# A four-layer kernel on one core: the next norm's transposes moved from TensorE to eight DMAs, and the first two up products of an element done together

## What is computed

```python
x = x + (ctx @ Wo + bo)                 # end of the first pass; x2 below
h = _ln(x) * g2 + beta2                 # h2 below: "the next norm"
ff = _gelu2(h @ W1 + b1) @ W2 + b2      # 512 -> 2048 -> 512; first half of the steps
x = x + ff                              # x3 below

h = gelu(x @ Wi[e] + bi[e])             # layer 3, weights of expert e of the element
r = h @ Wo[e] + bo[e] + x               # second half of the steps
y = norm(r) * gamma[e] + beta[e]        # f below

Af, Bf = A_grid * y, B_grid * y         # layer 4: a stencil step on the 512 x 512 grid
out = max(y + dt * (-grad(Af) + 0.5 * grad2(Bf)), 0)
```

## Time and profile before

| | us |
|---|---|
| median of three timed runs | 2524.64 |
| lowest, highest | 2522.03, 2525.68 |
| the profiled execution | 2522.23 |
| span from its first to its last instruction | 2520.4 |
| TensorE busy, share | 2471.3, 98% |
| VectorE busy, share | 1904.1, 76% |
| ScalarE busy, share | 1126.5, 45% |
| GpSimd busy, share | 981.1, 39% |
| TensorE in the chain that ended last | 52% |

### The profile page before, as it was taken

How to read it: one execution, slowest core, us unless ns; L and a number is a source line. 1 busy time by engine, 2 the same in 40 slices (tenths; PEclk the granted TensorE clock), 3 DMA queues, 4 the chain that set the end, 5 groups by cost and what they waited for, 6 DMA issues and landing times.

```text
span 2520.4 us, 45559 instructions
## 1 busy us (share of the span) xinstructions
PE 2471.3 (98%) x14444; PEld 1221.4 (48%) x14444; DVE 1904.1 (76%) x3666; ACT 1126.5 (45%) x2159; POOL 981.1 (39%) x840
## 2 busy tenths in 40 slices
PE   7999999999999999999999999999999999999997
PEld 5555555555555555544444444444444444444443
DVE  7878777777777685763588689678787886986777
ACT  3666767675758585742223223233222322232231
POOL 1464646464646464410044143242341440531331
PEclk9999999999999999999999999999999999999999
DMA  7444444544544445451232142133222322321341
GB/s 244 140 154 155 152 156 152 164 153 151 166 149 161 148 151 169 159 193 51 72 126 84 62 135 92 59 117 117 84 87 92 105 84 75 125 92 59 114 140 53
DMA packets 150228, 311.35 MB, mean 124 GB/s; under 512 B 16619, under 2 KB 21739, under 8 KB 150004
## 3 DMA queue, kind: packets, MB, share of 16 engines
q1 hardware_dynamic: 140788, 291.93, 35.4%
q10 hardware_dynamic: 9216, 16.78, 1.8%
HBM read 291.68 MB, written 16.81 MB: 122 GB/s over the span
## 4 chain that ended last, share of the span: by engine, by line
PE 52%; DVE 3%; issue 1%; ACT 0%; POOL 0%; DVEq 0%; ACTq 0%
PE bank L1522 17%; PE bank L1524 16%; PE bank L1523 16%; PE bank L1508 1%; PE bank L1598 1%; DVE g2T_hi L1857 1%; DVE g2T_lo L1858 1%; PE bank L1528 0%; DVE w_hi L1933 0%; ACT g L1690 0%; DVE stage L1820 0%; DVE stage L1801 0%; PE bank L1644 0%; PE bank L1632 0%; DVE w_lo L1933 0%
## 5 line engine op out<-in xcount | busy, mean ns | idle before, releaser
L1109 DVE CUSTOM_DVE_ANT_0 w_words<-bank,stage 128x512 f32<-128x512 f32 x512 | 323.8, 686 | 102.0 <-PE bank L702 93.7
L884 ACT ACTIVATE w_words<-w_words,nmax 128x512 f32<-128x512 f32 x512 | 363.6, 714 | 42.1 <-DVE nmax L1109 41.0
L564 POOL TENSOR_TENSOR stage<-stage,mask_add 128x1024 f32<-128x1024 f32 x128 | 273.1, 2144 | 230.1 <-DMA stage<-in_bias 213.2
L1857 DVE CAST g2T_hi<-g 128x512 f16<-128x512 f32 x256 | 178.8, 698 | 221.0 <-ACT g L1690 217.1
L725 PE MATMUL bank<-ident,w_words 128*128 128x128 f32 x2048 | 298.3, 280 | 11.6 <-DVE late L1124 5.9
L725 PEld LDWEIGHTS bank<-ident,w_words 128*128 128x128 f32 x2048 | 222.8, 140 | 170.8 <-issue 82.9
L1690 ACT ACTIVATE g<-bank,bi 128x512 f32<-128x512 f32 x128 | 88.0, 687 | 352.3 <-PE bank L1524 331.3
L1858 DVE TENSOR_TENSOR g2T_lo<-g,g2T_hi 128x512 f16<-128x512 f32 x256 | 238.7, 933 | 8.8
L1432 POOL TENSOR_TENSOR stage<-grid,f 128x512 f32<-128x512 f32 x84 | 141.3, 1708 | 195.5 <-DVE f L1760 74.0
L870 ACT ACTIVATE late<-bank 128x512 f32<-128x512 f32 x256 | 150.9, 590 | 147.4 <-PE bank L725 147.2
L1866 DVE SCALAR_TENSOR_TENSOR wl_lo<-stage,wl_hi 128x1024 f16<-128x1024 f32 x128 | 196.6, 1536 | 6.8 <-ACT wl_hi L1702 6.6
(11 more groups left out here) (299 smaller groups left out, 4894.8 us busy)
## 6 DMA issues: line engine op xcount, KB each, us to landing
stage<-in_bias SPq DMA_DIRECT2D x256, 512.0 KB, 4.4
stage<-in_W_l SPq DMA_DIRECT2D x128, 512.0 KB, 3.4
grid<-in_grids SPq DMA_DIRECT2D x140, 256.0 KB, 3.6
xin<-in_x SPq DMA_DIRECT2D x32, 256.0 KB, 4.1
x_rows<-w_words ACTq DMA_DIRECT2D x32, 256.0 KB, 3.7
out<-stage ACTq DMA_DIRECT2D x32, 256.0 KB, 2.0
late<-x_rows SPq DMA_DIRECT2D x7, 1024.0 KB, 8.3
l_rows<-in_rows SPq DMA_DIRECT2D x8, 768.0 KB, 6.2
```

Of the source, the lines that this page charges most:

```text
L564: pool.tensor_tensor(bias[:, n % NB, :, :], bias[:, n % NB, :, :], mask_add[:, u % T, :].unsqueeze(1).to_broadcast([P, 2, S]), ALU.add).th ...
L884: act.activation(tile, tile, ACT.Exp, scale=-1.0, bias=nmax[:, u % 2, i:i + 1], accum_out=rsum[:, j, h:h + 1]).then_inc(prob_ready, 1)
L1109: dve.tensor_tensor_reduce(tiles[:, 4 * (u % NR) + i, :], bank[:, :], bias[:, half % NB, i % 2, :], -1.0, 3.0e38, ALU.add, ALU.min, nmax[: ...
L1857: link(dve.tensor_copy(gT[0][:, n % 4, :], g32[:, n % 2, :]))
```

## The change

The transposes of `h2` are taken from TensorE and given to DMAs that transpose on the way from SBUF to SBUF.

- ScalarE makes the high half of `h2` in rows, in float16, in steps 26 and 27 (two row tiles each), VectorE the low half in steps 27 and 28. They lie in `stage`, where `prod` lies (`h2_halves`).
- SP, at the end of its sequence for the element, waits for these and for the end of `up(31)` (the last reader of `xT`), and issues eight transposing DMAs: the four row tiles of the high half, then the four of the low half. Each moves 128 x 512 values of 16 bit. Each half has its own semaphore.
- The ring loses the four `h2T` entries.
- TensorE does `down(28)` to `down(31)` all after `up(31)`. Before, `down(28)` and `down(29)` stood behind `up(30)` and `up(31)`.
- TensorE does `up(0)` and `up(1)` of the next element together (`first_ups`): after the high halves are there, the 16 products that need only `xT` high, 8 for each bank; after the low halves are there, the 4 products with `xT` low for `up(0)` and then the 4 for `up(1)`.
- GpSimd waits for both halves before it writes `prod`.
- Semaphores are merged (`zeroed` into the new one of the split).

```diff
@@ end of SP's sequence(it)
+                if not is_last(it):
+                    sp.wait_ge(h2_split_and_zeroed, 1 + it * T + T)
+                    arrived(sp, it, ("up", STEPS - 1))
+                    sp.sem_inc(carrier, 1)
+                    for half in range(2):
+                        for t in range(T):
+                            sp.dma_start(xT[half][:, :, t * P:(t + 1) * P], h2_halves[half][:, t, :], transpose=True)\
+                                .then_inc(h2T_in[half], 16)
@@ GpSimd
                 if not is_first(it):
+                    for half_in in h2T_in:
+                        pool.wait_ge(half_in, it * 64)
                     for t in range(T):
                         alpha_products(pool, it - 1, t)
@@ TensorE
-                            elif not is_first(it):
-                                pe.wait_ge(h2T_split, it * C)
...
+                def first_ups():
+                    ws = [[[x[:, c, n * P:(n + 1) * P] for x in w1] for c in range(C)] for n in range(2)]
+                    first = [claim(pe, it, ("up", n)) for n in range(2)]
+                    pe.wait_ge(h2T_in[0], it * 64)
+                    for n in range(2):
+                        for c in range(C):
+                            pe.matmul(first[n][:, :], ws[n][c][0], xT[0][:, c, :], start=c == 0, stop=False)
+                            pe.matmul(first[n][:, :], ws[n][c][1], xT[0][:, c, :], start=False, stop=False)
+                    pe.wait_ge(h2T_in[1], it * 64)
+                    for n in range(2):
+                        for c in range(C):
+                            mm = pe.matmul(first[n][:, :], ws[n][c][0], xT[1][:, c, :], start=False, stop=c == C - 1)
+                        mm.then_inc(full_of(("up", n)), 1)
...
                     for n in range(half * NF, half * NF + NF):
-                        up(n)
-                        if n - LAG_DOWN >= half * NF and not (is_last(it) and n - LAG_DOWN >= STEPS - KEPT):
+                        if n == 0 and not is_first(it):
+                            first_ups()
+                        if n > 1 or is_first(it):
+                            up(n)
+                        if half * NF <= n - LAG_DOWN < STEPS - KEPT:
                             down(n - LAG_DOWN)
...
-                    if half:
-                        pe.wait_ge(h2_ready, it * T + T)
-                        for c in range(C):
-                            h2_transposes(claim(pe, it, ("h2T", c)), c).then_inc(full_of(("h2T", c)), 1)
-                    for n in range(half * NF + NF - LAG_DOWN, half * NF + NF):
+                    for n in range(STEPS - KEPT if half else NF - LAG_DOWN, half * NF + NF):
                         down(n)
@@ ScalarE
-                for c in range(0 if is_last(it) else C):
-                    copy_hi(("h2T", c), c)
+                    if n in (NORM2 + 3, NORM2 + 4) and not is_last(it):
+                        if n == NORM2 + 3:
+                            act.wait_ge(y_done, 1 + it * T)
+                            if is_first(it):
+                                act.wait_ge(w_split, len(PIECES))
+                        for t in range(2 * (n - NORM2 - 3), 2 * (n - NORM2 - 2)):
+                            act.wait_ge(h2_ready, it * T + t + 1)
+                            act.activation(h2_halves[0][:, t, :], h2[:, t, :], ACT.Copy).then_inc(hi_done, 1)
@@ VectorE
+                    if n in (NORM2 + 4, NORM2 + 5):
+                        for t in range(2 * (n - NORM2 - 4), 2 * (n - NORM2 - 3)):
+                            dve.wait_ge(hi_done, it * (C + T) + C + t + 1)
+                            dve.wait_ge(h2_ready, it * T + t + 1)
+                            dve.tensor_tensor(h2_halves[1][:, t, :], h2[:, t, :], h2_halves[0][:, t, :], ALU.subtract)\
+                                .then_inc(h2_split_and_zeroed, 1)
                 if is_last(it):
                     return
-                for c in range(C):
-                    lo_of(("h2T", c), C + c, c, h2T_split)
```

More of the change, by code:

```diff
@@ L1192, in ffn_pass @@
             in_ring(("L3", STENCIL[n]))
-    for c in range(C):
-        in_ring(("h2T", c))
     banks = Banks(order)
@@ L1217, in ffn_pass @@
         h2 = sb("h2", [P, T, D], F32)
+        h2_halves = [stage[:, 2 + i, :].bitcast(F16).rearrange("p (t d) -> p t d", t=T) for i in range(2)]
         f = sb("f", [P, T, D], F32)
@@ L1244, in ffn_pass @@
         ident_set = sem("ffn_ident_set")
-        zeroed = sem("zeroed")
         x2_in = sem("x2_in")
@@ L1253, in ffn_pass @@
         hi_done = sem("ffn_hi_done")
-        h2T_split = sem("h2T_split")
+        h2_split_and_zeroed = sem("h2_split_and_halo_zeroed")
+        h2T_in = [sem("h2T_hi_in"), sem("h2T_lo_in")]
         x3T_split = sem("x3T_split")
@@ L1310, in claim @@
             k = last[1]
-            signal, per = {"h2T": (h2T_split, C), "x3T": (x3T_split, C), "up": (gelu_ready, STEPS),
+            signal, per = {"x3T": (x3T_split, C), "up": (gelu_ready, STEPS),
                            "L3": (sum_ready, T)}[last[0]]
@@ L1396, in load_halo @@
                     sp.wait_ge(alpha_done, it * T)
-                    sp.wait_ge(zeroed, 1)
                     for k, part in enumerate((*vsp, *msp)):
@@ L1454, in _ @@
                                pattern=[[-1, P]], channel_multiplier=1).then_inc(ident_set, 1)
-            pool.memset(halo[:, :, :].rearrange("p t d -> p (t d)").bitcast(F32), 0.0).then_inc(zeroed, 1)
+            pool.memset(halo[:, :, :].rearrange("p t d -> p (t d)").bitcast(F32), 0.0).then_inc(h2_split_and_zeroed, 1)
             pool.wait_ge(cols_in, 16 * len(cols))
@@ L1524, in three @@
                 return pe.matmul(out, w[1], x[0], start=False, stop=last)
-            def h2_transposes(bank, c):
-                for t in range(T):
-                    mm = pe.transpose(bank[:, t * P:(t + 1) * P], h2[:, t, c * P:(c + 1) * P], ident[:, :])
-                return mm
             pe.wait_ge(sh["hT_split"], (B + 1) * C)
@@ L1837, in lo_of @@
                 def lo_of(key, k, c, signal):
-                    dve.wait_ge(hi_done, it * 2 * C + k + 1)
+                    dve.wait_ge(hi_done, it * (C + T) + k + 1)
                     dve.tensor_tensor(xT[1][:, c, :], psum[banks.place[key][0]][:, :], xT[0][:, c, :], ALU.subtract)\
```

## The result

The changed kernel takes 2532.47 us against 2524.71 us for the kernel before, medians of eight runs each made side by side: a ratio of 1.0032, 95% interval 1.0020 to 1.0043. It is slower, by 7.8 us. One of the changed kernel's eight runs fell in a slow state at a lower clock (3724.94 us); ratio and interval are of the fast ones, and the seven alone have a median of 2532.35 us, 7.6 above. The prediction was 2523.5 us and no measurable change; the change came out slower by a cost that stands in none of its steps. The time lies inside the stated range of 2514 to 2558 us, but the range reached so far up for low halves that come late, and TensorE never waited for them: that it holds is luck. The profiled execution took 2531.22 us, with a span of 2529.4 us, 9.0 more than before.

The account below looks back on a forecast made before the run. TensorE was taken as the bound, busy 2471.3 of 2520.4 us. Six boundaries at -0.02 us and the last at -0.97 summed to -1.1 us, from 2524.64 to 2523.5 us; range 2514 to 2558 us.

Parts of the forecast that it names:

- step (1): At seven element boundaries the 16 transposes leave TensorE: -1.75 us each, -12.2 us if nothing else moved.
- steps (2) and (3): Moving down(28) and down(29) behind up(31), and the h2 copies to steps 26 to 28, costs nothing.
- step (4): On SP, weight chunks and grids queued behind the transposes still land in time for their users; no cost.
- step (5): After up(31), high halves land at 4.2 us and low ones at 6.7, before they are wanted: no wait.
- halo row: Profile row of an SBUF-to-SBUF copy, 0.59 us to issue, 1.7 to landing, taken as the transposing DMAs' price.
- first rival: SP's transposes do not overlap, low halves come 4.6 us late at each boundary: +32 us, 2556 us; chance 0.26.
- steps (6) and (7): up(0) fills 1.73 us later, delaying down(2) by 1.73 at six boundaries and 0.78 at the last.
- The shift is absorbed: Rival: VectorE has room for up(0)'s later completion, so the transposes' gain stays: 2511 us; chance 0.09.
- either of the two new waits: Sign of being wrong: TensorE standing in first_ups for the high or the low halves; no wait was forecast.

Follow-up runs that it names:

- e6: Changed kernel with TensorE's loop head at slot 16, first loads ahead of the transposes, up(0)'s low products right after its eight high ones: 2510.78 us, ratio 0.9954.
- e1: Changed kernel with only the head of TensorE's loop put back at slot 16 of a code block: 2527.16 us, ratio 1.0012.
- e2: Kernel before, without transposing DMAs, with only the head of TensorE's loop moved to slot 238: 2530.05 us, ratio 1.0029.
- e5: Changed kernel with TensorE's loop head at slot 16 and the next element's first loads issued ahead of the transposing DMAs: 2521.03 us, ratio 0.9994.
- e3: Kernel before, transposes still on TensorE, with the new joint order of up(0) and up(1) and the loop head at slot 16: 2534.18 us, ratio 1.0043.
- e9: Changed kernel with TensorE's loop head at slot 16 and VectorE's at slot 0, loads still behind the transposes: 2522.14 us, ratio 0.9994.
- e4: Changed kernel with TensorE's loop head at slot 16 and up(0)'s low products after 12 high products instead of 16: 2529.18 us, ratio 1.0017.
- e10: Kernel before with the next element's first loads held until up(0) is full and four semaphore increments ahead of VectorE's loop: 2529.42 us, ratio 1.0026.

## Why the prediction failed

**The transposes, step (1): the amount right, its condition not.** TensorE's busy time fell by 10.9 us in the trace, and e6 brings 11.3 net. But the step says "-12.2 us if nothing else moved", and then looked only for work that moved. What moved was the code: some 33 instructions taken from the element ahead of the loop carried the loop's head from slot 16 to about 239, and each of five jumps back fetches nine blocks. That is the step that failed: a term put at nothing that cost 9.8 us in the trace (e1 takes it away, e2 brings it into the kernel before), and it is the whole miss: -1.1 + 9.8 = +8.7 against a measured +7.8. The profile's page of before had a row for it, queue 8 with 98 packets, and so had the diff, in what it removes; none of the rivals was about it.

**The moved downs and the copies, steps (2) and (3): right.** No gap before `down(28)` to `down(31)`, and no new wait of TensorE on a split in those steps.

**SP's order, step (4): right for the data, incomplete.** TensorE and GpSimd have no new wait for the chunks and grids. The step asked only who uses the data. It did not ask what else is on the DMA engines at the new time; there VectorE's code is. In the changed kernel that stays hidden; in e1 it cost 2 us of waits, with the half clock on top.

**The DMA transposes, step (5): no wait, as forecast, but the size off by two.** They do not overlap as the halo row suggested, 0.62 us apart: they are issued 1.3 us apart, each of 128 KB, and land after 2.5 us at the median, from this view of the changed kernel's line 1417 (ns to issue, min/median/max; then landing):

```profile
L1417 SPq DMA_TRANSPOSE hT_hi<-stage x28: 1242/1261/1313, 1240.8 to 2306.1; - x28
L1417 SPq DMA_TRANSPOSE hT_lo<-stage x28: 1251/1268/2242, 1246.1 to 2311.3; - x28
...
DMA to landing us min/median/max: 2.5/2.5/5.0
```

By their semaphores the high halves are in 6.6 us after the last up product at every boundary. The low ones are in 11.8 us after it in e1 and e5 (12.7 and 12.8 at the first boundary). Wanted were they at 10.2 and 13.65. The halo row gave 4.2 and 6.7, the first rival 9.2 and 18.4: its mechanism is half real, and a slack of under 2 us decided against it. In the changed kernel even that slack is not there. At the five boundaries with a fetch the low halves land at 13.5 to 15.2, at three of them past 13.65, and TensorE doesn't wait for them only because the fetch holds it up for longer.

The Trainium skill, Advanced Engine Details and Errata, section X-Bar Transpose, gives 350 to 400 GB/s for transposing DMAs. The trace disagrees for this use: 1 MB in 10.7 us of issue is about 100 GB/s. The Trainium skill, VectorE: DVE Perf Modes, section The three transpose paths, gives 1309 ns for a 128x128 block by DMA. Taken as a rate the trace disagrees, as 1261 ns is what four such blocks take to issue here; the landing of one such DMA, 2.5 us, is of four blocks, and no run here has a single one.

**The shift of up(0), steps (6) and (7): right.** +1.73 us forecast for each of six `down(2)`, from 0.17 to 1.90; measured 1.77 (once 1.83), 0.11 of the difference now standing before `down(0)`. For the last boundary 0.78 was forecast and 0.45 measured, a term a little too large. The table load begins 6.14 us after the first product in the rows above, 4.6 without the 1.53 of the fetch, as forecast. e3 measures the part alone: +11.1 us, where the steps give 6 x 1.73 + 0.78 = 11.2. "The shift is absorbed" falls with it.

**The sum.** e5, the change without either code effect, gives -1.1 us by the medians, the sum of the steps. That it agrees to the tenth is luck: the interval runs from -3.8 to +0.8 us. "I am wrong if TensorE stands at either of the two new waits" was nearly met in the wrong way: it stood at the first of them and a few products beyond, and not for the wait.

## What to carry over

When a change adds or removes instructions ahead of a loop, compare where the loop's head and its last block fall before pricing anything else, and look at the instruction queues' rows for packets in later bodies; a loop head pinned to a slot saved some 4 us here for TensorE alone (7.8 above before, then 4.1 in e1) and 9 for TensorE and VectorE together (e9 is 1.4 below before). A gap released by "issue", in the middle of a row of equal instructions, behind a jump back, was a code fetch here on both engines, and large loads moved onto that moment made it longer on VectorE, so loads without a deadline belong ahead of it. Splitting a computation by what arrives first helps only if the group that starts the next engine's chain is still completed first: high halves of one group, then its low halves, then the next group, was worth 10 us over all high halves first.

## What the runs showed of the hardware

- **Code position.** A loop of TensorE of 1709 instructions ran without a packet with its head at slot 16 and was fetched anew, nine packets of 16 KB per jump, with it at slot 238: +6.9 us in five jumps (e2). The first pass's loop of 2067 instructions is fetched in every round, ten packets each. That seven blocks fit and eight do not is my reading of two positions in two bodies, not a scan of all.
- **Transposing DMAs land later beside a code fetch.** The eighth transpose lands 11.8 us after the last up product where TensorE fetches nothing (e1) and 13.5 to 15.2 us after it where it does (changed kernel).
- **VectorE fetches in every body.** Its queue 14 has 43 packets of 8 KB in the second pass of the kernel before, of the changed one and of e2. At a jump the packets start 2.4 us apart, and 4.9 us apart behind 1.8 MB of loads (e1).
- **The clock.** e1 ran two stretches of 3.4 us at the lower level, 1.2 GHz, each right behind a wait of TensorE before `down(2)` (2.17 and 2.46 us late). Timeline of TensorE and granted clock of a window around it (us, PE busy, ..., PEclk 0.83):

```profile
1622.85 0.39 PE L1530 MATMUL bank<-w_hi,g2T_hi 128*128 128x512 f16 x1 [2.01 <-DVE g2T_lo L1878]
...
1623.71 0.63 PE L1530 MATMUL bank<-w_hi,g2T_hi 128*128 128x512 f16 x1
1624.14 0.63 PE L1531 MATMUL bank<-w_lo,g2T_hi 128*128 128x512 f16 x1
```

```profile
1618.00:1628.00 10.00, 7.99 (x30) 3.09 (x28) 9.86 (x12) 0.63 (x1) 4.63 (x3) 0.83 0.22 79
```

  Products lie 0.43 us apart there instead of 0.216, which costs about 1.7 us a time. e4 has four such stretches, behind waits of 2.26 to 2.83 us; the changed kernel, e3, e5, e9 and e10, late by 1.83 us at most, have none in the loop. e1 also has one boundary late by 2.25 us without one, so the length of the gap alone does not decide, and what does stays open.
